# First attention stage of a fused four-layer kernel: from one unit at a time to four units in row tiles of 32

## The reference, cut to what matters

```
latent = rmsnorm(x @ W_kv) * g_kv                     # 32 numbers for each token
k = [latent @ W_kdec (8 per head), rope(x @ W_krope) (32 per head)]
q = [x @ W_q @ W_qdec (8 per head), rope(x @ W_q @ W_qrope) (32 per head)]
v = latent @ W_vdec                                   # 16 heads of 8
y = softmax(causal(q k^T / sqrt(40))) v @ W_o         # 16 heads
x = x + y
```

## Time and profile before

| | |
|---|---|
| time, median of 3 runs | 3694.22 us (3691.56 to 3694.41) |
| the profiled execution: its own time | 3693.26 us |
| its span, first to last instruction | 3691.4 us |
| TensorE, VectorE, ScalarE, GpSimd busy over the span | 83%, 58%, 46%, 35% |
| mean granted TensorE clock | 0.912 |

### The profile page before, as it was taken

How to read it: one execution, slowest core, us unless ns; L and a number is a source line. 1 busy time by engine, 2 the same in 40 slices (tenths; PEclk the granted TensorE clock), 3 DMA queues, 4 the chain that set the end, 5 groups by cost and what they waited for, 6 DMA issues and landing times. The chain is left out here.

```text
span 3691.4 us, 76433 instructions
## 1 busy us (share of the span) xinstructions
PE 3077.6 (83%) x21672; PEld 2178.5 (59%) x21673; DVE 2127.0 (58%) x7924; ACT 1697.9 (46%) x5110; POOL 1295.3 (35%) x1492
## 2 busy tenths in 40 slices
PE   5999999968788718378986997699998999999656
PEld 4666666635455505257764665366666677777546
DVE  3666666645688832278875555655554555555464
ACT  1544444422455403156653665255546666666310
POOL 2444444400677630357761332222213222222110
PEclk6999999989899959789998999799999999999765
DMA  2000000023000011100000000000000000000000
GB/s 59 1 1 1 0 0 1 0 62 100 18 0 0 7 67 36 46 28 0 0 13 17 0 0 0 1 1 0 0 18 5 2 1 0 0 1 0 3 0 23
DMA packets 41212, 47.35 MB, mean 13 GB/s; under 512 B 6224, under 2 KB 30760, under 8 KB 40776
## 3 DMA queue, kind: packets, MB, share of 16 engines
q1 hardware_dynamic: 38992, 41.33, 3.9%
q0 software_dynamic: 2048, 4.20, 0.4%
HBM read 35.40 MB, written 10.12 MB: 12 GB/s over the span
## 5 line engine op out<-in xcount | busy, mean ns | idle before, releaser
L735 ACT ACTIVATE a_pr<-a_sm,a_top 128x256 f32<-128x256 f32 (+1 forms) x1024 | 455.2, 445 | 555.5 <-DVE a_top L602 536.1
L602 DVE CUSTOM_DVE_ANT_0 a_sm<-bank,cst 128x256 f32<-128x256 f32 (+1 forms) x1024 | 315.2, 355 | 333.6 <-PE bank L494 288.2
L1725 POOL TENSOR_TENSOR a_sm<-a_sm,a_top 128x512 f32<-128x512 f32 x384 | 389.7, 1040 | 122.2 <-DVE a_top L1548 122.1
L494 PE MATMUL bank<-a_kx,a_q 128*128 128x512 f32 (+7 forms) x1120 | 409.6, 471 | 11.4 <-POOL a_kx L816 8.3
L1654 ACT ACTIVATE a_pr<-a_sm 128x512 f32<-128x512 f32 x384 | 240.4, 629 | 148.4 <-POOL a_sm L1725 130.3
L816 POOL TENSOR_TENSOR a_kx<-a_k,cst 128x512 f32<-128x512 f32 (+1 forms) x238 | 273.3, 1161 | 100.2 <-ACT a_k L1003 92.2
L506 PEld LDWEIGHTS bank<-cst,a_pr 128*128 128x128 f32 x1536 | 189.4, 141 | 134.7 <-issue 114.0
L494 PEld LDWEIGHTS bank<-a_kx,a_q 120*128 120x128 f32 (+2 forms) x1120 | 208.2, 194 | 96.8 <-issue 70.1
L527 PE MATMUL bank<-a_pt,a_v 128*32 128x128 f32 (+1 forms) x3072 | 236.3, 284 | 0.1
L506 PE MATMUL bank<-cst,a_pr 128*128 128x128 f32 x1536 | 233.6, 274 | 0.0
L826 POOL COPY a_rx<-a_rden 128x512 f32<-128x512 f32 (+1 forms) x64 | 52.7, 824 | 483.9 <-DVE a_rden L624 400.2
(11 more groups left out here) (443 smaller groups left out, 6948.2 us busy)
## 6 DMA issues: line engine op xcount, KB each, us to landing
f_spread<-gate_rows SPq DMA_DIRECT2D x16, 512.0 KB, 7.6
W<-in_l_w SPq DMA_DIRECT2D x2, 2048.0 KB, 10.0
x_sorted<-p_zero SPq DMA_DIRECT2D x4, 768.0 KB, 5.5
f_xin<-x_sorted SPq DMA_DIRECT2D x12, 256.0 KB, 3.0
y_sorted<-f_yout SPq DMA_DIRECT2D x10, 256.0 KB, 2.3
X<-in_x SPq DMA_DIRECT2D x4, 512.0 KB, 7.1
a_bias<-bias_rows SPq DMA_DIRECT2D x1, 2048.0 KB, 7.7
out_x<-X SPq DMA_DIRECT2D x8, 256.0 KB
```

Of the source, the lines that this page charges most:

```text
L494: mm = pe.matmul(sbank[s % 2][:, (h - h0) * kw:(h - h0 + m) * kw], B["q"][b][0:rows, c, qt * P:(qt + 1) * P], B["kx"][b][0:rows, h:h + m, ...
L602: ins = dve.tensor_tensor_reduce(sm[s % R][:, h * kw:(h + 1) * kw], sbank[s % 2][:, h * kw:(h + 1) * kw], mk, 1.0, 3.0e38, ALU.add, ALU.mi ...
L735: ins = act.activation(pr[s % R][:, h * kw:(h + 1) * kw], src[:, h * kw:(h + 1) * kw], ACT.Exp, bias=top[:, qt, h0 + h:h0 + h + 1], scale= ...
L1725: pool.tensor_tensor(whole, whole, top[:, qt, a:a + m].unsqueeze(2).to_broadcast([P, m, kw]), ALU.subtract).then_inc(S["shifted"], 1)
```

## The change

The first attention stage calls `narrow_stage` in place of `attention_stage`. Its heads are laid out as `L0_HEADS`: heads r, r+4, r+8 and r+12 share the row tile r. A unit's scores are now accumulated: one matmul of 32 content rows over all 512 columns, then one matmul of 32 rope rows for each head (four of 128 columns in slot 0, two of 256 in slots 1 and 2). Rope rows need no spreading; the content rows are spread once, in one instruction. The steps are 12: the RMS factors, the content rows of q and of k, four chunks of 128 rope rows of q, four of k, and v. Since there are now four steps to a slot, `narrow_stage` gives them four places in it, one each, in place of "all but the last" in the middle and the last at the end. In the other two narrow stages, with one step for each slot, that one stays at its end. The row sums come from the column of ones. The folding stage has five products in place of seven, and the weights are smaller.

```diff
-class LatentSteps(Steps):
...
-        self.kinds = ["pre"] + ["q"] * 6 + ["k"] * 6 + ["v"]
-        self.engine = ["dve"] * 14
...
+L0_HEADS = Narrow(
+    8, 2,
+    early=[[r, r + 4, r + 8, r + 12] for r in range(4)],
+    late=[[r + i, r + i + 4] for i in (0, 8) for r in range(4)],
+    place=lambda h: (h % 4 * 32, 32, h // 4, h // 4),
+    column=lambda h: (h // 8, h % 4, h // 4 % 2))
...
+        def steps_at(s, place):
+            k = place - 4 + len(at_quad[s % NQ])
+            return at_quad[s % NQ][k:k + 1] if k >= 0 else []
...
+                if steps.content:
+                    for j in range(4):
+                        qt, heads, kw = units[4 * q + j]
+                        r0, rows, c, x = hd.place(heads[0])
+                        pe.matmul(sbank[j][:, :], B["qc"][b][r0:r0 + rows, qt * P:(qt + 1) * P],
+                                  B["kc"][b][r0:r0 + rows, x:x + len(heads), 0:kw], start=True, stop=False)
...
-                                   B["kx"][b][r0:r0 + rows, x:x + m, 0:kw], start=True, stop=True)
+                                   B["kx"][b][r0:r0 + rows, x:x + m, 0:kw],
+                                   start=not steps.content, stop=not steps.content or heads[-1] == all_heads[-1])
...
             def slot(i, s):                      # TensorE
                 if in_loop(i):
                     scores(i, s)
+                    steps_in(i, s, 0)
                 for q in lagging(i, s, LV):
                     values(i, q)
+                if in_loop(i):
+                    steps_in(i, s, 1)
                 for q in lagging(i, s, LT):
                     turn(i, q, 0)
                     turn(i, q, 1)
                 for e in ending(i, s, LY):
                     project(i, s, e)
...
+                    steps_in(i, s, 2)
                 (denominators, repeat_turn, turns 2 and 3)
...
+                    steps_in(i, s, 3)
...
             def slot(i, s):                      # VectorE
                     mask(i, s, 0)
                     mask(i, s, 1)
+                    steps_in(i, s, 0)
                 copies(i, s, (0, 1))
                     mask(i, s, 2)
+                    steps_in(i, s, 1)
                     mask(i, s, 3)
                 (residual, recip, norm, keep_moments)
+                    steps_in(i, s, 2)
                 copies(i, s, (2, 3))
                 (tile_stats)
+                    steps_in(i, s, 3)
...
+class LatentNarrow(NarrowSteps):
+        self.kinds = ["rms", "cq", "ck"] + ["q"] * 4 + ["k"] * 4 + ["v"]
+        self.engine = ["act", "act", "dve"] + ["dve"] * 9
...
+    def wait_q_and_k(self, pe, S, seq):
+        pe.wait_ge(S["k_ready"], seq + 1 + CREDIT)
+        pe.wait_ge(S["rope_added"], 8 * (seq + 1) + CREDIT)
+        pe.wait_ge(S["step_out"], 12 * seq + 2 + CREDIT)
...
-        hd = Heads(16, 40, 8, [(0, P), (0, SEQ)], causal=True)
-        attention_stage(core, ctx, 0, hd, LatentSteps(rkv, F), Epilogue(weight(core, 0, "l0_wo")),
-                        next_weights=next_weights)
+        narrow_stage(core, ctx, 0, L0_HEADS, LatentNarrow(L0_HEADS, rkv, F), Epilogue(weight(core, 0, "l0_wo")),
+                     next_weights=next_weights)
```

More of the change, by code:

```diff
@@ L107, in shape_constants @@
     return out, np.ascontiguousarray(np.concatenate(resident, 1)), staged
-STAGED = {"rope40q": 0, "content40": 0, "rope40k": 0, "rope8q": 2, "rope8k": 2, "bucket": 2, "future": 2, "before": 5}
+STAGED = {"rope32q": 0, "ones": 0, "rope32k": 0, "rope8q": 2, "rope8k": 2, "bucket": 2, "future": 2, "before": 5}
 class Core:
@@ L1043, in l3_attention @@
                     next_weights=next_weights, ghost="l3_ghost")
-class LatentSteps(Steps):
-    roped = True
-    def __init__(self, rkv, F):
-        self.kinds = ["pre"] + ["q"] * 6 + ["k"] * 6 + ["v"]
-        self.engine = ["dve"] * 14
[L1056 to L1110, removed]
@@ L1135, in _ @@
             pe.wait_ge(gained, 2 + CREDIT)
[L1136 to L1139, removed]
+            pe.matmul(bank[0][:, 0:P], w("l0_wqT"), w("l0_wqall")[:, 0:P], start=True, stop=True)
+            pe.matmul(bank[1][:, :], w("l0_wqT"), w("l0_wqall")[:, P:], start=True, stop=True)
+            pe.matmul(bank[2][:, :], w("l0_wqT"), w("l0_wqrot"), start=True, stop=True)
+            pe.matmul(bank[4][:, 0:P], w("l0_wkvT"), kdec[:, :], start=True, stop=True)
             pe.matmul(bank[6][:, 0:P], w("l0_wkvT"), vdec[:, :], start=True, stop=True).then_inc(products, 1)
@@ L1147, in _ @@
             dve.wait_ge(products, 1 + CREDIT)
[L1148 to L1152, removed]
+            dve.tensor_copy(F["q"][:, 0:P], bank[0][:, 0:P])
+            dve.tensor_copy(F["q"][:, P:], bank[1][:, :])
+            dve.tensor_copy(F["qrot"][:, :], bank[2][:, :])
+            dve.tensor_copy(F["kc"][:, :], bank[4][:, 0:P])
             dve.tensor_copy(F["v"][:, :], bank[6][:, 0:P])
@@ L1502, in _, with steps_in @@
                 step(0, 0, j, True)
+            def steps_in(i, s, place):
+                for j in steps_at(s, place):
+                    step(i, s // NQ + 1, j)
             def slot(i, s):
@@ L1514, in slot @@
                 if in_loop(i):
-                    for j in at_quad[s % NQ][:-1]:
-                        step(i, s // NQ + 1, j)
+                    steps_in(i, s, 2)
                 for e in ending(i, s, LD):
@@ L1524, in slot @@
                 if in_loop(i):
-                    for j in at_quad[s % NQ][-1:]:
-                        step(i, s // NQ + 1, j)
+                    steps_in(i, s, 3)
             all_quads(pe, slot)
@@ L1763 @@
     ropes = 0
+    content = False
     def alloc(self, sb, sem, B, S):
@@ L3225, in lay_out @@
     o = {}
-    head_cat = lambda c, r: np.concatenate([c.reshape(-1, 16, 8), r.reshape(-1, 16, 32)], 2).reshape(-1, 640)
-    zero = lambda rows, d: np.zeros((rows, 16 * d), np.float32)
+    content = lambda w: w.reshape(-1, 4, 4, 8).transpose(0, 2, 1, 3).reshape(-1, P)
     o["l0_wkv"], o["l0_wkvT"], o["l0_wqT"] = v["L0_attn_W_kv"], v["L0_attn_W_kv"].T, v["L0_attn_W_q"].T
```

95 lines of the change are left out of this document (76 added, 19 removed), and 6 rows, old and new, of the table WEIGHTS.

## The result

The changed kernel takes 3687.86 us (median of 20 runs, 3679.31 to 3695.26) against 3694.41 us (20 runs, 3691.27 to 3698.36): ratio 0.9981, 95% interval 0.9975 to 0.9988. The forecast was 3622 us, range 3555 to 3690; so a gain of 71 us was expected and 6.5 came.

The account below looks back on a forecast made before the run. The prediction took the old first stage to be bound by TensorE and the new one by its chain of waits. 3693.3 less 59 (walk), 10.4 (head), 4 (fold), plus 3 (tail) gave 3623, stated as 3622 us; range 3555 to 3690.

Parts of the forecast that it names:

- The walk: First attention stage's loop over 16 sequences: 36.8 us each, 589 in all against 648.1, 59 us less.
- the idle ahead of the copy: First stage, slot 1: VectorE waits 2.4 us before copying turn 1; named as a sign at some 2 us.
- the third product released by GpSimd: First stage, slots 1 and 2: the third step's product on VectorE waits for GpSimd's addition, behind four shifts.
- Slot 0: First stage's slot with steps rms, cq, ck, q0: laid out at 9.5 us.
- The 0.45 a sequence added for the loop: First stage's walk: added to the slots' 36.35 us, after the third stage laid out at 19.65 against 20.2 traced.
- the waits that the prediction named for q3 and k3: First stage: product q3 waits for q1's addition (to 11.65 us); scores after slot 2 wait for k3's (to 13.25).
- The copy of the moments: Copy at L1587: takes 1.00 us beside a running shift, for two elements.
- Head, fold, tail: Around the first stage's walk: head 15.6 against 26.0 us, 10.4 less; fold 4 less; tail 3 more.
- engines (3453): Rival: engines, not the chain, set the first stage's time, 419 us for 16 sequences; below 3540 has chance 0.05.
- longer trips: Rival: each first-stage slot needs 1.5 us more than laid out, gain gone, 3693; chance 0.11 for 3660 to 3700.
- tiles in turns: Rival: accumulating row tiles take turns, a quad's scores 6.8 us in place of 1.95, 3855 in all; chance 0.02.
- the clock: Rival: TensorE's clock falls in the first stage's walk, with TensorE some 70% busy, making it slower; chance 0.10.

Follow-up runs that it names:

- experiment 1: Changed kernel with idle filler instructions ahead of the third stage's loop (69 VectorE, 68 ScalarE, 21 GpSimd), putting later loops at their old places: 3622.21 us.
- experiment 2: Changed kernel with the 69 filler instructions on VectorE alone, ahead of the third stage's loop: 3620.12 us.
- 3: Changed kernel with the 68 filler instructions on ScalarE alone, ahead of the third stage's loop: 3690.15 us.
- 4: Kernel before, with fillers (187 VectorE, 188 ScalarE, 235 GpSimd) bringing its later loops to the changed kernel's places modulo 256: 3785.79 us.
- experiment 7: Changed kernel with VectorE fillers (20 ahead of the first stage's loop, 49 ahead of the third's) and four rope product buffers instead of two: 3587.86 us.
- experiment 5: Changed kernel with 69 VectorE fillers, 20 ahead of the first stage's loop and 49 ahead of the third's: 3620.05 us.
- 10: Changed kernel without fillers, with a VectorE prefetch hint in the attention loops naming the branch back to the top: 3622.85 us.
- experiment 6: Changed kernel with 197 VectorE fillers ahead of the third stage's loop, 128 more than 69: 3621.67 us.
- experiment 9: Changed kernel without fillers, with an alignment directive on VectorE loading each attention loop's first instruction at a block's start: 3620.21 us.
- 12: Kernel before, with the alignment directive ahead of VectorE's attention loops and nothing of the change: 3671.81 us.
- 8: Changed kernel with 69 VectorE fillers, first stage's sixteen rope matmuls of a slot issued bank by bank instead of alternating row tiles: 3651.18 us.

## Why the prediction was wrong

- **The step that failed** is the sentence "The two other narrow stages keep their order, so nothing is counted there", and with it that nothing at all was counted for what comes behind the first stage. Order and work did stay. The place of VectorE's loops did not, and that cost 11.5, 33.1 and 28.2 us, the last in a stage that the prediction doesn't mention. Shown by experiments 1 and 2 (put back, the time is 3622 and 3620), 3 (ScalarE's place gives nothing) and 4 (the loss alone).
- **How the gaps cost more than themselves.** In the fifth stage VectorE's issue gaps sum to 24.0 us and the stage loses 33.1. TensorE idles behind them:

```profile
1701.89 1.15 PE L1377 MATMUL bank<-a_kx,a_q 32*128 32x256 f32 x16
...
1707.63 1.16 PE L1423 MATMUL bank<-W,a_on 128*128 128x128 f32 x8 [2.56 <-DVE a_top L1503]
...
1710.12 1.12 PE L1440 MATMUL bank<-cst,a_rx 128*128 128x128 f32 x4 [1.32 <-DVE a_top L1503]
```

  The mean granted clock falls from 1.00 to 0.95 and the same matmuls are busy 308 us instead of 291. With the directive it is 1.00 and 291 again. In the last attention stage 17.1 us of gaps cost 28.2, with 12.2 us more of TensorE busy; in the third, where TensorE has more slack, 13.6 cost 11.5. How much of the excess is the clock was not separated by a run of its own.
- **The walk, right:** 587.5 against 589 laid out (means of slots 1 and 2 13.3 and 13.5 against 13.5 and 13.35; scores 1.93 against 1.95, the content part 0.96 where 1.07 was taken and the rope part 0.97 where 0.89 was, and no run shows how much of either goes to filling and changing tiles; the idle ahead of the copy 2.18 against some 2; the third product released by GpSimd). Slot 0 was laid out with 9.5; inside an iteration it takes 9.7, at the loop's edge 9.7 to 11.3, in the mean 10.0. The 0.45 a sequence added for the loop covers that (the check on the third stage would have asked for 0.55, 1.6 us more in all). The chain is confirmed by experiment 7, whose gain of 32 us is near the sum of the waits that the prediction named for q3 and k3, 29.5. TensorE was busy 77%, where about 70% was named, at 0.96, just under the 0.97: these two signs were missed.
- **The copy of the moments** takes 1.00 us in the prediction's row of the third stage. In the new stage it isn't slow at all: all 29 in the changed walk take 0.16 to 0.22 us, where in the third stage before 14 of 29 took 1.0.
- **Head, fold, tail, right:** the head 16.5 against 15.6 (51.87 to 68.38), with a granted clock of 0.50 from 50 to 60 us and 0.90 from 60 to 65; the fold 3.4 less against 4 (its end at 27.30 against 30.70); the tail 11.6 against 12.9. The stage as a whole gained 71.7, the sum forecast 70.4.
- **Right partly by luck.** "TensorE is busy 630 of 649 us", and so "bound by TensorE", hid that VectorE's refetching lay on the path of the old stage: without it the stage ends 23.6 us earlier, with TensorE busy for 621 of 625. The gain of 71.7 in the first stage is 51.4 of the change itself and 20.3 of an old refetch that the new form hides in VectorE's slack (23.6 less the 3.3 that the new stage gives back, itself within the spread of experiment 5). The forecast was laid out for the new stage and read from the trace for the old, so it needed no knowledge of this.
- **The rivals:** engines (3453), longer trips and tiles in turns didn't come; the clock in the first stage's walk stayed at 0.96, where the old stage's was at 0.98. The clock did fall, but in other stages, and as a consequence: with the loops put back by the directive the third and the fifth are at 0.99 and 1.00 again. No rival named a cost outside the changed stage. That 3687.86 lies under the range's upper end of 3690 is luck: that end was set for longer round trips (3660 to 3700, chance 0.11), which did not come.

## What to carry to other kernels

When a change shortens or lengthens the program of an engine, every loop behind it moves. Compare stage by stage, not in the sum: suspect the place where a stage's code didn't change and its time did, and issue gaps stand at its loop edges. More packets on the instruction queue support that, but an equal count doesn't rule it out, as the last attention stage shows (39 and 39). Give long loops on VectorE a fixed place or a hint on the branch back before measuring anything else (here one directive, worth 68 us on the changed kernel and 22 on the one before), and put two versions on the same footing before they are compared.

And an engine that is 97% busy (TensorE in the old first stage) does not show that nothing else is on the path: that stage gave 24 us when VectorE's fetching went away.

## What the runs showed of the hardware

- A loop of 285 to 378 instructions on VectorE is either held (5 to 9 packets on the queue in a whole walk, where ScalarE's loop is held too) or fetched anew in its seven iterations (36 to 39 packets), by its place, or by whether the branch back is announced (10). The price is a gap of up to 3.1 us at the loop edge; for the whole stage 1.6 us an iteration in the third (11.5 / 7), 4.7 in the fifth, 4.0 in the last, and next to nothing in the changed first stage. The same place shifted by 128 instructions behaves the same (6), and all lengths are held with the directive: 285 to 347 in experiment 9, 378 in 12.
- A packet on the queue is of 8 KB and holds some 128 instructions of VectorE: 128 fillers more bring one packet more (91 in experiment 6, 90 in experiment 2). The places speak for blocks of 128 as well. In the trace of the changed kernel the fifth stage's loop (285 instructions) begins 924 instructions of VectorE behind the third's (297), each loop counted once, and both are fetched anew. If a loop is held only where three such blocks contain it (the author's assumption; no run shows the three), the third's is not contained from places 88 to 127 of a block and the fifth's from 100 to 127; 924 is 28 more than a multiple of 128, so both can be so at once. This is an inference from counts: where exactly the border lies was not measured.
- ScalarE's loops (111 to 230 instructions, its accumulator reads not counted) and GpSimd's (50 to 110) moved as well and cost nothing that shows: 3690.15 with ScalarE's alone put back. The 230 of the last attention stage are fetched anew in experiment 1 and not in experiment 2 (38 and 8 packets), and the stage takes 694.4 and 694.8 us.
- Sixteen 32-row matmuls of 128 columns take 1.07 us when the row tiles alternate and 2.71 when each tile's four follow each other (8, a single run).
